# Rewriting the order of work at the opening, at the phase change and at the end of a post-norm transformer layer

## The reference, cut to what matters

```
q, k, v = rope(x@Wq.T+bq), rope(x@Wk.T+bk), x@Wv.T+bv      # reshaped to (B, S, H=16, D=32)
att = softmax(einsum('bshd,bstd->bsht', q, k) / sqrt(D))
out = einsum('bsht,bstd->bshd', att, v); out = swapaxes(out, 1, 2).reshape(B, S, E) @ Wo.T + bo
x = layernorm(x + out)
g = (x @ gate_w.T) * gate_s; u = (x @ up_w.T) * up_s        # 512 -> 1408
x = layernorm(x + ((silu(g) * u) @ down_w.T) * down_s)
```

## Time and profile before

| | us |
|---|---|
| median of the runs | 1778.35 (the two undisturbed ones: 1778.27 and 1778.35) |
| the profiled execution | 1778.3 |
| its span, first to last instruction | 1776.5 |
| PE busy in it | 1716.8 (97%) |
| DVE, ACT, POOL busy | 1383.4, 942.1, 812.9 |

### The profile page before, as it was taken

The page is one execution under the profiler, slowest core; times in us unless marked ns, Lnnn a source line. Parts: engine busy times, 40 slices in busy tenths (PEclk is TensorE's granted clock), DMA queues, the critical chain, the costliest instruction groups (busy, mean ns, idle before and its releaser), DMA issues.

```text
span 1776.5 us, 40766 instructions
## 1 busy us (share of the span) xinstructions
PE 1716.8 (97%) x15138; PEld 1406.2 (79%) x15138; DVE 1383.4 (78%) x1980; ACT 942.1 (53%) x1457; POOL 812.9 (46%) x697
## 2 busy tenths in 40 slices
PE   7889999999999999999799999999999999999997
PEld 5767888888888888888578888888888888888885
DVE  7878999998999999998756766677676776767756
ACT  4545556545655555465535455554555545555453
POOL 5778888888888888887300110201102011020112
PEclk9989999999999999999899999999999999999999
DMA  6585776787677767868674452644526445254341
GB/s 190 104 171 142 164 178 165 153 179 176 159 153 177 173 161 163 179 166 195 186 243 134 134 165 84 206 151 133 171 81 202 151 134 170 90 194 151 96 165 71
DMA packets 447191, 278.06 MB, mean 157 GB/s; under 512 B 261408, under 2 KB 385696, under 8 KB 447136
## 3 DMA queue, kind: packets, MB, share of 16 engines
q1 hardware_dynamic: 447136, 277.37, 58.5%
HBM read 183.97 MB, written 93.32 MB: 156 GB/s over the span
## 4 chain that ended last, share of the span: by engine, by line
PE 91%; issue 2%; DVE 2%; SPq 2%; POOL 1%; DMA 1%; ACT 1%; POOLq 0%; ACTq 0%; DVEq 0%
PE ps_x L599 13%; PE ps_x L603 12%; PE ps_x L600 12%; PE ps_s L755 9%; PE ps_s L760 8%; PE ps_x L755 7%; PE ps_x L760 7%; PE ps_x L766 4%; PE ps_x L770 4%; PE ps_s L671 3%; PE ps_a L633 2%; PE ps_s L766 2%; PE ps_a L766 2%; PE ps_a L770 2%; PE ps_s L770 2%
## 5 line engine op out<-in xcount | busy, mean ns | idle before, releaser
L599 PE MATMUL ps_x<-wqkv_hi,xc_hi 128*128 128x512 f32 x768 | 305.6, 398 | 18.6 <-POOL xc_lo L1127 8.0
L603 PE MATMUL ps_x<-wqkv_hi,xc_lo 128*128 128x512 f32 x768 | 301.6, 393 | 0.0
L600 PE MATMUL ps_x<-wqkv_lo,xc_hi 128*128 128x512 f32 x768 | 301.6, 393 | 0.0
L1261 POOL TENSOR_TENSOR z<-z,xr 128x512 f32<-128x512 f32 x62 | 79.7, 1310 | 483.9 <-DVE z L1575 483.9
L755 PE MATMUL ps_s<-x_hi,slot 128*128 128x512 f32 x672 | 264.9, 394 | 3.1 <-DVE hid L1508 2.1
L760 PE MATMUL ps_s<-x_lo,slot 128*128 128x512 f32 x672 | 262.2, 390 | 0.0
L901 ACT ACTIVATE kX<-kT 32x512 f32<-32x512 f32 x256 | 160.8, 628 | 168.8 <-DVE kT L1346 166.5
L1149 POOL TENSOR_TENSOR qk_cos<-qk_in,rot 128x512 f32<-128x512 f32 x128 | 204.1, 1594 | 79.7 <-DVE qk_in L1323 58.2
L755 PE MATMUL ps_x<-x_hi,slot 128*128 128x512 f32 x560 | 220.0, 393 | 7.4 <-ACT x_hi L1058 4.8
L760 PE MATMUL ps_x<-x_lo,slot 128*128 128x512 f32 x560 | 218.9, 391 | 0.0
L1155 POOL TENSOR_TENSOR qk_cos<-qk_cos,qk_sin 128x512 f32<-128x512 f32 x128 | 203.9, 1593 | 10.7 <-DVE qk_sin L1330 0.7
(11 more groups left out here) (116 smaller groups left out, 3730.9 us busy)
## 6 DMA issues: line engine op xcount, KB each, us to landing
slot<-gu_hi SPq DMA_DIRECT2D x88, 896.0 KB, 5.0
xc<-x_cols SPq DMA_DIRECT2D x32, 512.0 KB, 5.5
v_rows<-v_in SPq DMA_DIRECT2D x32, 512.0 KB, 4.3
v<-v_rows SPq DMA_DIRECT2D x32, 512.0 KB, 5.2
res<-x_rows SPq DMA_DIRECT2D x64, 256.0 KB, 3.6
x_rows<-x_out SPq DMA_DIRECT2D x32, 512.0 KB, 2.8
x_cols<-x_turn SPq DMA_DIRECT2D x128, 128.0 KB, 2.6
wide<-x_cols SPq DMA_DIRECT2D x64, 256.0 KB, 5.1
```

The source lines that it names most:

```text
L599: pe.matmul(out, hi[:, k], w_hi[w][:, k], start=(k == 0), stop=False)
L600: pe.matmul(out, hi[:, k], w_lo[w][:, k], start=False, stop=False)
L603: last = pe.matmul(out, lo[:, k], w_hi[w][:, k], start=False, stop=(k == KE - 1))
L1261: pool.tensor_tensor(z[:, h, r], z[:, h, r], xr[:, r], ALU.add).then_inc(z_added[h], 1)
```

## The change: what it does

- **Opening, all engines.** PE computes the second tile of unit 1 before the scores of unit 0, and generally keeps `score` and `weigh_values` apart: no call of one directly follows the other. The two halves of `project_heads` can be called apart (`rows`). DVE, ACT, POOL and SP get new orders; slab 2 is summed in step 4 and no longer before it. The rope table of unit 2 is loaded after unit 0 is rotated (unit 1 has a table of its own), no longer after unit 1, and `load_x(3)` and `load_rope(3)` go ahead of slab transfers.
- **Steps 4 and 32** (straight). PE puts `weigh_values` between the two halves of `project_heads`. In step 4 the slab's sums, high and low part go between the rotations, and on SP the stores of x1 go ahead of the slab's DMAs.
- **Step 32 and the change of phase.** POOL adds the second output bias before the last slab's sums, and makes `first_sums_of_x` before them too. DVE leaves tile 1 of `add_residual(29)` for later and puts the first `low_of_x`, `low_of_heads(30)` and the rest before the flag; `subtract_top(31)` goes behind the flag. ACT interleaves `high_of_x` with the last slab.
- **The end.** The last rows' residual is loaded into `raw[:, 0]`, early (at j == 6), in place of `xr` once that is free. The last four chunks of `down2` go row by row (`by_rows`), so that rows 0 to 2 are complete earlier. DVE takes statistics of finished rows as they come.

The diff, cut:

```
@@ sync
-                    at_least(sp, rotated[w], 2 * m)
+                    at_least(sp, rotated[w], 2 if m == 2 else 2 * m)
...
+            store_v(0); load_x(2); ffn_slabs(1); load_v(0); load_rope(2); load_residual(0)   # one call per line
+            store_v(1); load_x(3); ffn_slabs(2); load_v(1); load_rope(3); ffn_slabs(3); load_residual(1); store_v(2)
+            for s in range(OPENING, UNITS + 1):
                 step(s)
...
-                if j == NJ and is_last(n):
+                if j == 6 and is_last(n):
                     load_rows(n, 1)
@@ tensor
                 if (m := unit_of(s, 3, UNITS)) is not None:
-                    project_heads(s, m)
+                    project_heads(s, m, (0,) if straight else (0, 1))
                 if (m := unit_of(s, 2, UNITS)) is not None:
                     weigh_values(m)
+                if straight and (m := unit_of(s, 3, UNITS)) is not None:
+                    project_heads(s, m, (1,))
...
             project_qk(1, 0)
+            project_qk(1, 1)
             score(0)
-            project_qk(1, 1)
             project_v(1)
+            project_qk(2, 0)
             score(1)
-            project_qk(2, 0)
+            project_qk(2, 1)
             weigh_values(0)
-            project_qk(2, 1)
             project_v(2)
-            project_heads(3, 0)
+            project_heads(3, 0, (0,))
             weigh_values(1)
+            project_heads(3, 0, (1,))
             score(2)
...
+                def by_rows(n):
+                    for r, chunks in ((0, (7, 8, 9)), (1, (7,)), (0, (10,)), (1, (8, 9, 10)), (2, (7, 8, 9, 10)),
+                                      (3, (7, 8, 9, 10))):
+                        for j in chunks:
+                            if r == 0:
+                                inputs_of_down2(n, j)
+                            down2(n, j, (r,))
@@ scalar, opening: split_x(1, 0), split_x(1, 1) now stand before spread_k(0, 0); spread_k(1, 0) before exponent(0)
@@ scalar, super_step(0)
+                    high_of_x(0, P1)
                     high_of_heads(UNITS - 2)
+                    high_of_x(0, P2)
+                    high_of_slab(UNITS - 1)
+                    high_of_x(0, P5)
                     top_of_slab(UNITS - 1)
-                    high_of_x(0, P1)
-                    high_of_x(0, P2)
+                    high_of_x(0, P6)
+                    high_of_x(0, P7)
                     exponent(UNITS - 1)
@@ gpsimd, opening
-            for t in range(2):
-                rotate(1, t, 1)
-                rotate(1, t, 0)
+            rotate(1, 0, 1); rotate(1, 0, 0); rotate(1, 1, 1)
             low_x(2, 0)
+            rotate(1, 1, 0)
             low_x(2, 1)
+            rotate(2, 0, 1)
             sums_of_slab(0)
+            rotate(2, 0, 0)
             low_of_slab(0)
...
@@ gpsimd, after step 32
             first_sums_of_x()
+            sums_of_slab(UNITS - 1)
+            low_of_slab(UNITS - 1)
@@ vector, the new order behind sines(1, 1, 0) (in part)
+            sums_of_prob(0); add_bias(1, 1, 2); turn_k(1, 1); scale_prob(0); turn_q(1, 1)
+            add_bias(2, 0, 1); sines(2, 0, 1); turn_prob(0); add_bias(2, 0, 0); sines(2, 0, 0)
+            subtract_top(1); turn_k(2, 0); add_bias(2, 1, 1); sums_of_prob(1); sines(2, 1, 1); turn_q(2, 0)
+            low_of_heads(0); add_bias(2, 1, 0); low_of_weight(W_ORDER[3]); scale_prob(1); sines(2, 1, 0)
+            turn_prob(1); turn_k(2, 1); turn_q(2, 1); add_bias(2, 0, 2); add_bias(2, 1, 2)
+            add_residual(0); aggregate(0)
@@ vector, super_step(0)
                     low_of_x(0, P1)
+                    low_of_heads(UNITS - 2)
+                    add_residual(UNITS - 3, (1,))
+                    aggregate(UNITS - 3)
                     low_of_x(0, P2)
+                    low_of_x(0, P5)
+                    dve.wait_ge(lo_seen, SLABS)
+                    dve.tensor_reduce(lo_top1[:, :], lo_top[:, :], AX.X, ALU.max).then_inc(lo_reduced, 1)
+                    sum_t(0, 2)
                     dve.wait_ge(lo_joined, 1)
                     dve.tensor_scalar(inexact[0:1, :], ps_x[0][0:1, 0:1], 0.0, None, ALU.is_gt).then_inc(flag_set, 1)
...
+                    subtract_top(UNITS - 1)
@@ vector, last super step
+                    read_row(n, 1, 0); shifts(n, 0); read_row(n, 1, 1); stats_of(n, 1, 0)
+                    read_row(n, 1, 2); stats_of(n, 1, 1); add_row(n, 2)
```

More of the change, by code:

```diff
@@ L341, in is_last, with rows_of_x1 @@
             return isinstance(n, int) and n == SUPERS - 1
+        def rows_of_x1(n, h):
+            return raw[:, 0] if is_last(n) and h == 1 else xr
         def table_of(m):
@@ L856, in super_step @@
                     down1(n, NJ - 1)
-                    for j in range(1, NJ - 2):
+                    for j in range(1, 7 if is_last(n) and not with_lo else NJ - 2):
                         inputs_of_down2(n, j)
@@ L864, in super_step @@
                         down2(n, NJ - 1)
-                    else:
+                    elif not is_last(n):
                         inputs_of_down2(n, NJ - 1)
@@ L952, in step @@
             def step(s):
-                ending = isinstance(s, int) and s == UNITS
-                slabs(s)
+                late, ending = (isinstance(s, int) and s == n for n in (OPENING, UNITS))
+                if not late:
+                    slabs(s)
                 if (m := unit_of(s, 3, UNITS)) is not None:
                     high_of_heads(m)
+                if late:
+                    top_of_slab(s - 3)
                 if (m := unit_of(s, 2, UNITS)) is not None:
@@ L1185, in step @@
             def step(s):
-                ending = isinstance(s, int) and s == UNITS
+                late, ending = (isinstance(s, int) and s == n for n in (OPENING, UNITS))
                 if (m := unit_of(s, 4, UNITS)) is not None:
                     rstd_of(m)
-                if (m := unit_of(s, 2, UNITS)) is not None:
+                if (m := unit_of(s, 2, UNITS)) is not None and not late:
                     low_of_slab(m)
@@ L1401, in turn_x1, with add_residual @@
                        .then_inc(x1_turned, 1)
-            def add_residual(m):
-                for t in range(2):
+            def add_residual(m, rows=(0, 1)):
+                for t in rows:
                     dve.wait_ge(o_done, 2 * m + t + 1)
@@ L1488, in _ @@
             sines(1, 1, 0)
+            sums_of_prob(0)
+            add_bias(1, 1, 2)
+            turn_k(1, 1)
             scale_prob(0)
-            turn_k(1, 1)
+            turn_q(1, 1)
+            add_bias(2, 0, 1)
+            sines(2, 0, 1)
             turn_prob(0)
-            turn_q(1, 1)
-            add_bias(1, 0, 2)
-            add_bias(1, 1, 2)
-            low_of_weight(W_ORDER[3])
-            step(3)
+            add_bias(2, 0, 0)
+            sines(2, 0, 0)
+            subtract_top(1)
+            turn_k(2, 0)
+            add_bias(2, 1, 1)
+            sums_of_prob(1)
+            sines(2, 1, 1)
+            turn_q(2, 0)
+            low_of_heads(0)
+            add_bias(2, 1, 0)
+            low_of_weight(W_ORDER[3])
+            scale_prob(1)
+            sines(2, 1, 0)
+            turn_prob(1)
+            turn_k(2, 1)
+            turn_q(2, 1)
+            add_bias(2, 0, 2)
+            add_bias(2, 1, 2)
+            add_residual(0)
+            aggregate(0)
             unit_steps(dve, step, LAGS, UNITS, 1)
-            low_of_heads(UNITS - 2)
-            subtract_top(UNITS - 1)
-            dve.wait_ge(lo_seen, SLABS)
-            dve.tensor_reduce(lo_top1[:, :], lo_top[:, :], AX.X, ALU.max).then_inc(lo_reduced, 1)
             def sum_c22(n, j):
@@ L1664, in super_step @@
                 if now is None:
-                    add_row(last, 2)
-                    stats_of(last, 1, 0)
                     read_row(last, 1, 3)
                     add_row(last, 3)
-                    for r in range(1, 4):
+                    for r in range(2, 4):
                         stats_of(last, 1, r)
```

147 lines of the change are left out of this document (86 added, 61 removed).

## The result

The changed kernel took 1773.05 us (median of nine runs, 1770.8 to 1774.8) against 1778.89 for the kernel before (nine runs, one of which, 3898.4, stands far apart and hardly moves the median): ratio 0.997, 95% interval 0.9961 to 0.9979. The forecast was 1763.6. The sign was right. The gain was 5.8 us by the medians and 5.5 by the two profiled executions, where 14.7 were forecast. The profiled execution took 1772.8 and spans 1771.0.

A forecast was written before the change was run, and what follows sets the result against it. PE was taken to bound the kernel (91% of the span). Gains of 8.3 (opening, step 4, first pass), 4.5 (change of phase) and 1.9 (end), 14.7 in all, took 1778.3 to 1763.6 us; range 1751 to 1774.

The forecast's parts named there:

- with 12 long matmuls between I expect none: Steps 3, 4 and 32: the waits with no cause shown would vanish once long matmuls separate the streams of small instructions.
- What bounds the kernel: Whole kernel: PE bounds it, 91% of the span; 1502 us in the loop and second phase stay unchanged.
- The opening: Up to the end of unit 2's scores: PE's lead mostly lost waiting for V until 79.4; gain 0.4 us, ends -2 and 11.
- 79.4 + 1.5 + 3.7 + 1.9: Opening, behind the wait for V: weighing, second half of the heads and scores would end at 86.5.
- Step 4: Step 4: most waits and the uncaused gaps go, 27.1 us instead of 35.35; gain 8.2 us, ends 4 and 9.6.
- First pass: First pass of the loop: low part of heads 2.3 late, fetch gap 1.0 kept; 29.0 against 28.68, loss 0.3 us.
- Change of phase: Step 32 to chunk 1's first product: earlier flag, chunk 1 at 865.3 instead of 869.77; gain 4.5 us, ends 1 and 8.
- The end: Behind the last matmul: last shift at 1769.0 for 1770.91, earlier statistics by rows; gain 1.9 us, ends 0.5 and 2.8.
- rival 1: Opening's gain is eaten: half clock covers 2 us more, step 4 saves 5 instead of 8.2; 1769 us, chance 0.25.
- rival 4: The uncaused gaps stay in step 4 and step 32; 1767.5 us, chance 0.07.
- rival 3: Loop locks into a worse phase of DVE and POOL, PE stopping in each of 26 units; 1790 us, chance 0.05.
- rival 2: No new stop in the opening: all four waits and their half clock go; 1749 us, chance 0.13.

The follow-up runs named there:

- experiment 2: Kernel after, with load_v(1) on SP moved ahead of the DMAs of slab 1: 1773.28 us.
- experiment 12: Kernel after, with 128 waits for a long-given semaphore ahead of PE's first product, shifting its later instructions against their blocks: 1776.75 us.
- experiment 1: Kernel after, with both halves of project_heads(3, 0) in the opening again ahead of weigh_values(1): 1771.96 us.
- experiment 5: Kernel after, with the work on slab 2 (high part, sums, low part) pulled forward in step 4: 1771.03 us.
- experiment 7: Kernel after, with the edits of experiment 1, experiment 2, experiment 5 and experiment 4 together: 1766.77 us.
- experiment 13: experiment 5 (slab 2 early) with the 128 extra waits of experiment 12 ahead of PE's first product: 1771.26 us.
- experiment 8: Kernel before, with the end's edits alone (last residual rows into the raw x buffer, last four chunks by rows): 1777.11 us, ratio 0.9995.
- experiment 9: Kernel before, with only the load of the last unit's V moved behind the first weight slots of the second phase: 1777.42 us.
- experiment 4: Kernel after, with the load of the last unit's V moved behind the first two weight slots of the second phase: 1769.52 us.
- experiment 10: experiment 7, with ScalarE's spreading of the opening's last keys moved ahead of the high part of slab 1: 1765.11 us.
- experiment 11: experiment 10, with the heads of step 4 in one piece while step 32 keeps its split: 1767.57 us.
- experiment 3: Kernel after, with the split of project_heads undone in steps 4 and 32 only: 1773.92 us.
- experiment 6: experiment 4, with two unused 512 KB copies between DRAM buffers put where the load of V had been: 1772.47 us.

## Why the forecast was wrong, step by step

Three steps failed: what follows the stop in the opening (half clock and a gap, 4.4 us), "with 12 long matmuls between I expect none" in step 4 (3.5), and the 4.7 us from flag to product taken as a constant (2.7).

- **What bounds the kernel**: right. The loop is unchanged within 0.1 us, all from P7 of chunk 0 to the last matmul within 0.5.
- **The opening** (gain 0.4 forecast, loss 4.0 measured): what ends the stop was right. The ends of DVE's list (74.99 for 75.3) and of V's load (79.36 for 79.4) came within 0.3 us. PE's own way there was not: the new wait of 2.92 at 49.41 is not in the forecast, PE was 5.6 us ahead at `project_qk(2, 1)` and not 8 to 9, and it stopped 5.28 us and not 7. This cost nothing, since V ended the stop. Wrong was the sum behind it, "79.4 + 1.5 + 3.7 + 1.9": the weighing took 4.2, with a gap of 1.78 for a block of instructions in it and half clock beside, the half of the heads 5.2, all at half clock (PE at 1.2 GHz from 78.2 to 88.4; only 1.0 was set down). The first end that I gave for this term, -2, was too near as well. Experiments 2 and 12 show the same sum without the gap: step 4 at 87.1 and 87.7.
- **Step 4** (8.2, measured 4.7): the waits were as forecast, 0.65 for 0.4 and 0.76 for 1.0. The step that failed is "with 12 long matmuls between I expect none": the gaps of the earlier trace rows did not vanish but moved, 2.5 us of them. With none inside its streams step 4 takes 27.7 (experiment 12), 3.0 less. The Trainium skill, Runtime: NRT & Kernel Launch, section Instruction fetch mechanics, has PE's instructions come by its own DMA queue in blocks of 16 KiB, and the refill mostly hidden. The first half agrees with the transfers of 16,384 bytes here; the second holds in streams of long matmuls, but not inside or right behind streams of 128 small ones (1.0 to 3.0 us in the rows above). I took from it that the gaps "would stay wherever they are", if they were not fetch. They were fetch, and did not stay.
- **First pass** (loss 0.3, measured gain 0.7): the term is near, by luck. Both of its waits came, at half their size: the low part of the heads 1.08 late for 2.3, the block's gap 0.57 for 1.0. The first is no constant: it was that short because PE came 8 us later than forecast. With PE earlier it was 2.45, 4.01 and 4.62 (experiments 1, 12 and 2), because the slab chain doesn't move with PE, and with the slab early it is gone (5, 7 and 13). So the sum of the first three parts, 8.3, which would have the next pass start at 142.5, is seen in no run with the slab in its new place. The earliest start there is 146.7 (experiment 1), and with PE 6.0 earlier (experiment 12) the pass ended no earlier. I followed the moved low part on GpSimd and DVE, but not on SP, where the load of the next slab waits behind it.
- **Change of phase** (4.5, measured 2.1): 1.2 are lost up to the flag, which comes 33.45 behind the start of step 32, not 32.2 (of this, the 0.81 ahead of the heads, for none: DVE's low part is later than forecast). 2.7 are lost in the term "from flag to first product it took 4.7 us on PE", which I took over as a constant. It is none: with idle DMA engines 4.7 to 4.9 (before, experiments 8, 9), with engines that are busy for less long 5.1 to 5.4 (4, 7, 10, 11), and 6.9 to 8.2 behind the slab's stores and V, or the copies (after, and 1, 2, 3, 5, 6, 12, 13). Two errors the other way hide part of this, which is luck: from the first product to P7 it took 7.0 us (7.1 before), where the forecast counts 7.6, and the 1.0 that it counts for the landing of slot 1 did not come. P6 and P7 on DVE, which I had feared for, cost nothing.
- **The end** (1.9): right, 2.4 less 0.5, and again 2.1 alone in experiment 8. That the figure fits to 0.1 is luck: the last shift came 4.5 us behind the last matmul where 5.0 were forecast, and from P7 to the last matmul PE took 0.5 longer where at most 0.3 were.
- **The rivals**: the cause was near rival 1 and rival 4 together, a gain eaten and gaps that stay. I gave them 1769 and 1767.5, each against the full 4.5 at the branch. The loop never changed its phase (rival 3), and 1749 (rival 2) was far.

Added up: 6.9 of the missing 9.2 us lie ahead of the loop, 2.4 at the change of phase, and the loop is 0.1 better. Experiment 10 (1765.1) shows that nearly the forecast's time can be had from the same operations, by the order of the slab, of the two loads of V, of the heads in the opening and of ScalarE. It beats both kernels.

## What to carry to other kernels

When a change takes waits from the engine that bounds a kernel, look for the slowest chain through the others in the same stage, each queue of DMA issues that a moved step releases included: that chain is the next floor, and of the gains above it half to all were lost here within one pass. A stop costs more than its length: behind the stops of 4.0 to 5.3 us PE ran at half clock, which cost 1.6 and 2.6 us in the heads of the first pass (experiments 12 and 2) and 2.4 in those of the opening. A duration between two marks (a flag and what follows) is a constant only as long as what runs beside it is the same; here, issuing a load that nobody waited for ahead of a branch cost 3.5 us behind the slab's stores, and nothing where the engines were idle (experiment 9). And a gap with no releaser is first to be held against the last rows of the engines that write its operands. If none ends there, and it lies in a stream of short instructions, it can be where a block of instructions arrives; one run with the code shifted tells it from a cost of the operation.

## What the runs showed of the hardware

- PE's instructions arrive in transfers of 16,384 bytes that take 0.9 to 1.8 us in these traces (two of 2.2 and 2.5). In streams of long matmuls PE didn't stop for them; inside or right behind streams of 128 small ones it stopped for 0.3 to 3.1 us and went on 1.2 to 1.5 us after the landing (1.05 once, in experiment 8). That a block is 256 instructions was my assumption for experiment 12; the run shows only that 128 more waits moved the gaps.
- The block behind the branch at the change of phase competes with data: its start came 2.0 to 2.6 us behind the flag with engines idle or soon idle, 3.7 to 5.0 with engines full, and PE's first product 1.6 to 1.7 behind its landing in every trace. How much of this is waiting in the engines and how much lies ahead of them the traces don't tell.
- The granted clock was half for 10.2 us around the stop that ended at 79.45 (78.2 to 88.4), for 3.4 or 6.8 us around others. What it costs hangs on how much of it falls into the stop: in experiment 6 it was half from 75.7 to 86.0, 3.2 us of this in the stop, for 1.3, and the half of the heads took 4.3 for 5.2. Which length it will be I can't say from these runs.
